# Two layers of graph attention on one core: moving a strip's side work of TensorE by one or two steps

## The chip, the cores and the metric

The kernel runs on one core of a Trainium2 chip. The metric is the device time of one execution in microseconds (us). Before the change it is 4260.31 us, the median of 3 runs (4258.36 to 4260.47).

## What is computed

The input `x` is 8 batches of 2048 nodes with 256 features, in float32, and `adj` is a 2048 x 2048 adjacency. Each layer adds its result to the normalized and rectified input's residual path.

```python
# layer 0
h = relu(layernorm(x))
q, k, v = h @ Wq.T + bq, h @ Wk.T + bk, h @ Wv.T + bv     # 4 heads of 64
scores = clip(q k^T / 8, -10, 10); masked entries are -10
attn = softmax(scores) within each of 8 chunks of 256 keys # per chunk
ctx = sum over the chunks of attn @ v
out = layernorm(ctx @ Wo.T + bo + h) * gamma + beta
x = x + out
# layer 1
h = relu(layernorm(x)); q = h @ W
attn = softmax(mask(leaky_relu(e_src[i] + e_dst[j])))      # over all 2048 nodes
x = x + elu(attn @ q)
```

The change touches only layer 0. What matters of it is that each of the 8 chunks of a row has a softmax of its own, so that each chunk's weighted sum must be divided by its own denominator before it is added to the others.

## The kernel before

Layer 0 (`layer0_block`) works batch by batch. A batch has 4 strips of 512 query rows (`NS`), and a strip has 32 steps (`STEPS`): one for each of 8 chunks of keys and 4 heads, in the order that `chunk_and_head` gives. At the start of a strip, steps 0 and 1 are heads 0 and 1, and head 2 is first met in step 4. Batch 0 is written out, batches 1 to 6 are a hardware loop, and batch 7 is written out.

In a step, TensorE makes the scores (`scores`, L674 and L675: four matmuls of 512 columns) into one of three PSUM slots. ScalarE takes the exponential in place (L829). VectorE clips it against the mask into one of four `probs` buffers (L968), which frees the slot. TensorE multiplies with the values (`values`, L687: 32 small matmuls) into one of two `outs` buffers. VectorE inverts the denominators (L974) and scales the sums into one of four `parts` buffers (L989), or directly into `ctx_sum` for chunk 0. GpSimd adds the part to `ctx_sum` (L514).

The order of the work on each engine is written out by hand. TensorE issues the scores of two steps and then, after the odd one, the values of the two steps that lie three and two behind. The values of a step wait until the sums of the step two before have been scaled. VectorE in step i first inverts and scales step i - 3 (`BACK`), then clips step i, and then does its side work of that step.

The three slots are used in one rotation (`count_uses`), by the scores and by all side work of TensorE, in the order in which TensorE issues it. Whoever wants a slot waits until the use three places before has been released by VectorE.

The side work of TensorE in a strip, each with one use of a slot:

- `turn` at step 3 and `project` at step 5 finish the strip before (transpose of `ctx_sum`, output projection).
- `transposes` (L596): a pair of tiles of the next batch's normalized input is transposed, and VectorE's `relu_t` (L893) brings it to `h_t`. `T_AT` gives the steps of the strip before's tiles in strips 1, 2 and 3, and `T_LAST_AT` those of the last strip's tiles, in strip 3. The last batch has none.
- `queries` (L624): the queries of the next strip for a pair of heads, in strips 0, 1 and 2, at the steps of `Q_AT`. ScalarE converts half of the result (L798), and VectorE the rest (L923), both standing in their engine's order right in that step. Then SyncE copies the two heads' halves to the other partitions with two DMAs (L397, `copy_queries`). The next strip's step 0 waits for the copies of heads 0 and 1, and its step 4 for those of heads 2 and 3.

GpSimd also makes the residual of each transposed pair (`residual`, L480 and L482), two steps ahead of `T_AT` by its own count.

The strips' side work that other engines have in the same steps stays at fixed steps: VectorE has statistics at 18 and 19, and normalizes tiles at 22 to 25 (strips 1 to 3), and in strip 0 at 18 to 21 and at 28 to 31.

Layer 1 (`layer1_block`) follows after layer 0 and holds none of the changed code.

Of the kernel before, what the change touches and what calls it, by code (L numbers as in the profile page):

```python
# [41 lines left out]
STEPS = NC * H  # L42
# [39 lines left out]
TURN_AT = 3  # L82
W_AT = 5
BACK = LAG + 1
T_AT = (26, 29)
T_LAST_AT = (10, 13)
Q_AT = (STEPS - 4, STEPS - 1)
GROUP = 2 * H
Q_AFTER_V = (3, 5)
W_MUL_AT = (8, 12)  # L90
# [23 lines left out]
def t_pairs(s):  # L114

    pairs = {}
    if s > 0:
        pairs.update({i: (s - 1, pair) for pair, i in enumerate(T_AT)})
    if s == NS - 1:
        pairs.update({i: (s, pair) for pair, i in enumerate(T_LAST_AT)})  # L120
    return pairs
# [7 lines left out]
def count_uses(last):  # L129
# [3 lines left out]
    def use(*name):  # L133
        place[name] = len(place)

    for s in range(NS):
        for i in range(STEPS):
# [5 lines left out]
            if i in t_pairs(s) and not last:  # L143
                use("t", *t_pairs(s)[i])
            if i in Q_AT and s < NS - 1:
                use("q", s + 1, Q_AT.index(i))
            if i in T1_AT and s == NS - 1 and last:
# [47 lines left out]
def layer0_block(nc, x, adj, wq_t, bq, wk_t, bk, wv_t, bv, wo_t, bo, gamma, beta, w, a, x1, mask_dram, s_dram, d_dram, both):  # L195
    with ExitStack() as ctx:
# [114 lines left out]
        def used(b, kind, *name):  # L311

            place = USES[kind][name]
            skipped = 2
            if kind == FIRST:
                skipped = sum(place >= USES[kind][(gone, 0)] for gone in ("turn", "project"))
            return b * BATCH_USES + PROLOGUE_USES - skipped + place

        def spot(kind, *name):

            return slots[used(0, kind, *name) % SLOTS]
# [9 lines left out]
        def acted(b, s, i):  # L331

            queries = sum(at < i for at in Q_AT) if s < NS - 1 else 0
            ahead_of_it = sum(at < i for at in P1_AT) if isinstance(b, int) and b == B - 1 and s == NS - 1 else 0
            return PROLOGUE_ACTS + b * BATCH_ACTS + s * STRIP_ACTS + i + queries + ahead_of_it + 1

        def acted_query(b, s, qu):

            return PROLOGUE_ACTS + b * BATCH_ACTS + s * STRIP_ACTS + Q_AT[qu] + qu + 2

# [13 lines left out]
        def tiles(s):  # L354

            return slice(s * IT, (s + 1) * IT)
# [88 lines left out]
        def _(pool):  # L445
# [24 lines left out]
            def inverse_std(n, strip):  # L470

                pool.wait_ge(moments_done, n)
                nc.gpsimd.tensor_tensor(rstd[:, strip], moments[:, strip, 1], eps_s[:, strip], ALU.add).then_inc(var_eps_done, 1)
                pool.wait_ge(var_eps_done, n)
                nc.gpsimd.tensor_tensor(rstd[:, strip], rstd[:, strip], neg_half[:, strip], ALU.pow).then_inc(rstd_done, 1)
# [41 lines left out]
            def batch(b, kind):  # L517
                first, last = kind == FIRST, kind == LAST
                for s in range(NS):
                    has_before = s > 0 or not first  # L520
                    before = (b, s - 1) if s > 0 else (b - 1, NS - 1)
                    for i in range(STEPS):
# [20 lines left out]
                        if s > 0 and not last:  # L543
                            if i == 17:
                                inverse_std(b * NS + s + 2, tiles(s - 1))
                            if i + BACK - 1 in T_AT:
                                pair = T_AT.index(i + BACK - 1)
                                pool.wait_ge(slot_filled, used(b, kind, "t", s - 1, pair) + 1)
# [20 lines left out]
        def _(pe):  # L569
# [50 lines left out]
            def queries(strip, qu, use, slot):  # L620

                fill(use)
                for c in range(KC):
                    last = nc.tensor.matmul(slot[:, 0, :], wq_s[:, c, qu * P:(qu + 1) * P],  # L624
                                            h_t[:, c, strip * STRIP:(strip + 1) * STRIP],
                                            start=(c == 0), stop=(c == KC - 1))
                last.then_inc(slot_filled, 1)
# [34 lines left out]
            def batch(b, kind):  # L662
# [30 lines left out]
                for s in range(NS):  # L693
                    has_before = s > 0 or not first
                    for i in range(STEPS):
# [11 lines left out]
                        if i in t_pairs(s) and not last:  # L707
# [4 lines left out]
                                       used(b, kind, "t", strip, pair), spot(kind, "t", strip, pair))  # L712
                        if i in Q_AT and s < NS - 1:
                            qu = Q_AT.index(i)
                            queries(s + 1, qu, used(b, kind, "q", s + 1, qu), spot(kind, "q", s + 1, qu))
# [1118 lines left out]
```

## Time and profile before

| | |
|---|---|
| time, median of 3 runs | 4260.31 us |
| the profiled execution's own time | 4262.97 us |
| its span, from the first to the last instruction | 4261.2 us |
| TensorE busy with matmuls | 91% |
| VectorE busy | 86% |
| ScalarE busy | 62% |
| GpSimd busy | 59% |
| mean granted TensorE clock | 0.987 |

The shares are averages over both layers. The last scores of layer 0 start at 2756.6 us of the span. The timeline of one engine shows when each instruction started and how long it took; a wait is printed in brackets behind the instruction that it held up, with the instruction that ended it.

### The profile page before, as it was taken

How to read it: one execution, taken by the hardware profiler on the slowest of the kernel's cores; microseconds unless marked ns; L12 is line 12 of the kernel's file. 1: busy time of each engine (PE TensorE's matmuls, PEld its weight loads, DVE VectorE, ACT ScalarE, POOL GpSimd, SP SyncE). 2: the span in 40 equal slices, each digit the busy share in tenths (PEclk: the TensorE clock that was granted, in tenths of full speed). 3: DMA queues.
4: the chain of work that ended last, by engine and by line, in shares of the span. 5: the costliest groups of instructions: out<-in, count | busy, mean ns of one | idle time of the engine just before them, and what ended most of it. 6: DMA issues, size and time to landing. Idle time of an engine off the chain costs nothing. (4 is left out here: it accounts for less than half of the span.)

```text
span 4261.2 us, 167542 instructions
## 1 busy us (share of the span) xinstructions
PE 3896.9 (91%) x72712; PEld 3242.9 (76%) x72712; DVE 3667.4 (86%) x6086; ACT 2656.7 (62%) x2960; POOL 2514.0 (59%) x1881
## 2 busy tenths in 40 slices
PE   6999999999999999999999999968889888888977
PEld 4877877777777777777787787757778787777877
DVE  5888888788788788788788888789999999999998
ACT  5665555555555555555565555457777777777776
POOL 4453554355345345354354353377988889888887
PEclk9999999999999999999999999989999999999999
DMA  6010010110101011010011010121221212122121
GB/s 129 29 30 23 27 32 22 37 32 22 34 26 32 27 32 32 28 27 27 22 37 32 22 30 22 34 66 26 87 70 43 85 35 82 55 61 75 40 67 38
DMA packets 170001, 178.75 MB, mean 42 GB/s; under 512 B 7184, under 2 KB 157072, under 8 KB 169104
## 3 DMA queue, kind: packets, MB, share of 16 engines
q1 hardware_dynamic: 166144, 156.08, 13.0%
q0 software_dynamic: 3088, 11.54, 1.3%
q8 instruction: 590, 9.67, 1.0%
q14 instruction: 179, 1.47, 0.1%
HBM read 107.02 MB, written 34.62 MB: 33 GB/s over the span
## 5 line engine op out<-in xcount | busy, mean ns | idle before, releaser
L829 ACT ACTIVATE slot<-slot,shift 128x1024 f32<-128x1024 f32 x1024 | 1077.2, 1085 | 931.4 <-PE slot L675 930.2
L514 POOL TENSOR_TENSOR ctx_sum<-ctx_sum,parts 128x256 f32<-128x256 f32 x896 | 651.0, 735 | 1325.5 <-DVE parts L989 1325.1
L968 DVE SCALAR_TENSOR_TENSOR probs<-slot,bound 128x1024 f32<-128x1024 f32 x1024 | 1242.7, 1217 | 94.2 <-ACT slot L829 88.3
L687 PEld LDWEIGHTS outs<-v_s,probs 128*64 128x64 f32 x32768 | 1007.5, 137 | 243.5 <-issue 166.6
L687 PE MATMUL outs<-v_s,probs 128*64 128x66 f32 x32768 | 1090.9, 223 | 42.7 <-DVE parts L989 31.0
L1597 ACT ACTIVATE t_ps<-s_all,d_rel 128x1024 f32<-128x1024 f32 x832 | 921.1, 1117 | 292.3 <-DVE p_dve L1710 277.4
L1710 DVE SCALAR_TENSOR_TENSOR p_dve<-t_ps,b_small,mask 128x1024 f32<-128x1024 f32 x832 | 1046.0, 1275 | 61.6 <-ACT t_ps L1597 60.6
L674 PE MATMUL slot<-q_hl,k_hl 128*128 128x512 f32 x2048 | 882.7, 431 | 28.5 <-DVE probs L968 21.0
L1439 POOL TENSOR_SCALAR p_pool<-r_all,b_big,b_small 128x1024 f32<-128x1024 f32 x192 | 746.5, 3888 | 141.7 <-ACT r_all L1589 141.6
L675 PE MATMUL slot<-q_hl,k_hl 128*128 128x512 f32 x2048 | 805.0, 393 | 0.0
L1500 PE MATMUL sums<-h_q_s,p_dve 128*64 128x66 f32 x13312 | 459.3, 226 | 113.9 <-DVE p_dve L1710 55.2
L1500 PEld LDWEIGHTS sums<-h_q_s,p_dve 128*64 128x64 f32 x13312 | 423.3, 140 | 156.1 <-DVE p_dve L1710 77.1
L674 PEld LDWEIGHTS slot<-q_hl,k_hl 128*128 128x128 f32 x2048 | 384.0, 188 | 149.8 <-DVE probs L968 39.8
L989 DVE TENSOR_TENSOR parts<-outs,inv 128x256 f32<-128x256 f32 x896 | 380.3, 424 | 120.5 <-POOL ctx_sum L514 34.8
L675 PEld LDWEIGHTS slot<-q_hl,k_hl 128*128 128x128 f32 x2048 | 385.4, 188 | 76.7 <-issue 11.5
L1442 POOL TENSOR_TENSOR p_pool<-p_pool,mask 128x1024 f32<-128x1024 f32 x192 | 411.1, 2141 | 16.0
L1500 PE MATMUL sums<-x_q_s,p_dve 128*64 128x66 f32 x6656 | 234.7, 229 | 73.5 <-DVE p_dve L1710 35.5
L789 ACT ACTIVATE bound<-mask,low 128x1024 f32<-128x1024 uint8 x256 | 293.9, 1148 | 0.8
L1500 PEld LDWEIGHTS sums<-x_q_s,p_dve 128*64 128x64 f32 x6656 | 218.1, 143 | 94.3 <-issue 40.7
L1500 PE MATMUL sums<-near,p_dve 128*64 128x66 f32 x6656 | 232.8, 228 | 53.1 <-DVE tail L1716 28.1
L1500 PEld LDWEIGHTS sums<-near,p_dve 128*64 128x64 f32 x6656 | 215.6, 142 | 71.0 <-DVE tail L1716 30.2
L798 ACT ACTIVATE q_hl<-slot,bq_s 64x512 fp32r<-64x512 f32 x128 | 87.4, 683 | 167.1 <-PE slot L624 166.3
(149 smaller groups left out, 4002.2 us busy)
## 6 DMA issues: line engine op xcount, KB each, us to landing
q_hl<-q_hl SPq DMA_DIRECT2D x128, 256.0 KB, 3.6
s_all<-s_turned SPq DMA_DIRECT2D x64, 512.0 KB, 5.6
x_q_s<-in_x SPq DMA_DIRECT2D x32, 512.0 KB, 4.7
x<-y SPq DMA_DIRECT2D x32, 512.0 KB, 3.1
t_o_s<-x SPq DMA_DIRECT2D x16, 1024.0 KB, 5.6
out<-t_o_s SPq DMA_DIRECT2D x16, 1024.0 KB, 8.5
x_q_s<-x SPq DMA_DIRECT2D x28, 512.0 KB, 7.1
probs<-in_adj POOLq DMA_DIRECT2D x12, 512.0 KB, 6.1
```

The source lines that it names most:

```text
L514: nc.gpsimd.tensor_tensor(ctx_sum[:, :, h, :], ctx_sum[:, :, h, :], parts[:, adds_before(i) % PARTS, :, :], ALU.add).then_inc(ctx_added, 1)
L674: nc.tensor.matmul(slot[:, r, :], kt, q_hl[:, h, 0, :], start=True, stop=False)
L675: end = nc.tensor.matmul(slot[:, r, :], kt, q_hl[:, h, 1, :], start=False, stop=True)
L687: end = nc.tensor.matmul(outs[i % OUTS][rows_of, q, 0:V_COLS], probs[:, i % PROBS, r, q * P + g * D:q * P + (g + 1) * D], v_s[:, c * JC + ...
L829: nc.scalar.activation(slot[:, :, :], slot[:, :, :], ACT.Exp, bias=shift[:, 0:1], scale=SCALE).then_inc(act_done, 1)
L968: nc.vector.scalar_tensor_tensor(probs[:, i % PROBS, :, :], spot(kind, "step", s, i)[:, :, :], P_LOW, bound[:, c % 2, :, :], ALU.max, ALU. ...
L989: nc.vector.tensor_tensor(parts[:, part % PARTS, :, :], outs[i % OUTS][:, :, 0:D], inv[:, i % 2, :].unsqueeze(2).to_broadcast([P, IT, D]), ...
L1439: nc.gpsimd.tensor_scalar(pp[:, n % PRING, :], r_all[:, m % HALVES, :], b_big[:, b % 2, j, h:h + 1], b_small[:, b % 2, j, h:h + 1], ALU.mu ...
L1442: nc.gpsimd.tensor_tensor(pp[:, n % PRING, :], pp[:, n % PRING, :], mask16[:, k, first:first + HALF], ALU.mult).then_inc(pp_made, 1)
L1500: last = nc.tensor.matmul(acc, left[:, t * P + g * D:t * P + (g + 1) * D], q_h, start=(j == 0 and t in (0, MAIN)), stop=(j == NT - 1), ski ...
L1597: nc.scalar.activation(t_ps[:, n % TRING, :], s_all[:, m % HALVES, :], ACT.Exp, bias=d_rel[:, b % 2, j, h:h + 1], scale=0.8).then_inc(t_ma ...
L1710: nc.vector.scalar_tensor_tensor(p[:, n % RING, :], t_ps[:, n % TRING, :], b_small[:, b % 2, j, h:h + 1], mask8[:, j, first:first + HALF], ...
```

## The change

Three tuples of step numbers change. All code that reads them follows: the order on TensorE, VectorE, ScalarE and GpSimd, the rotation of the slots and the semaphore counts.

```diff
@@ -82,9 +82,9 @@
 TURN_AT = 3
 W_AT = 5
 BACK = LAG + 1
-T_AT = (26, 29)
-T_LAST_AT = (10, 13)
-Q_AT = (STEPS - 4, STEPS - 1)
+T_AT = (25, 27)
+T_LAST_AT = (11, 13)
+Q_AT = (STEPS - 3, STEPS - 1)
 GROUP = 2 * H
 Q_AFTER_V = (3, 5)
 W_MUL_AT = (8, 12)
```

With it the two transposes of a strip move from steps 26 and 29 to 25 and 27, the first of strip 3's other pair from 10 to 11, and the first query projection from 28 to 29. The second projection stays at step 31. All of these are now odd steps, in which TensorE issues its side work after the values of a pair. VectorE's `relu_t` and both engines' conversions of the queries move with them, as do GpSimd's residuals (from steps 24 and 27 to 23 and 25).

## Rows read from the trace of the kernel before

**Rows 1.** The page: busy time (part 1), and a costly group (part 5: busy, idle, releaser).

```profile
PE 3896.9 (91%) x72712; PEld 3242.9 (76%) x72712; DVE 3667.4 (86%) x6086; ACT 2656.7 (62%) x2960; POOL 2514.0 (59%) x1881
...
L514 POOL TENSOR_TENSOR ctx_sum<-ctx_sum,parts 128x256 f32<-128x256 f32 x896 | 651.0, 735 | 1325.5 <-DVE parts L989 1325.1
```

**Rows 2.** Timeline of TensorE, end of a strip 2: start us, us, instruction, [idle before].

```profile
1305.36 0.50 PE L674 MATMUL slot<-q_hl,k_hl 128*128 128x512 f32 x1 [0.37 <-DVE probs L968]
...
1306.49 2.09 PE L687 MATMUL outs<-v_s,probs 128*64 128x66 f32 x64
...
1309.54 1.88 PE L624 MATMUL slot<-t_o_s,wide_s 128*128 128x512 f32 x4
...
1316.33 0.50 PE L674 MATMUL slot<-q_hl,k_hl 128*128 128x512 f32 x1 [0.45 <-DVE probs L968]
...
1319.47 1.98 PE L624 MATMUL slot<-t_o_s,wide_s 128*128 128x512 f32 x4
1320.89 0.80 PE L674 MATMUL slot<-q_hl,k_hl 128*128 128x512 f32 x1
...
1323.22 1.16 PE L687 MATMUL outs<-v_s,probs 128*64 128x66 f32 x32
1325.23 1.15 PE L687 MATMUL outs<-v_s,probs 128*64 128x66 f32 x32 [0.85 <-DVE parts L989]
1326.32 0.50 PE L674 MATMUL slot<-q_hl,k_hl 128*128 128x512 f32 x1
```

**Rows 3.** Timelines of VectorE and ScalarE in the same stretch.

```profile
1322.91 1.51 DVE L923 SCALAR_TENSOR_TENSOR q_hl<-slot,bq_s,q_hl 64x512 fp32r<-64x512 f32 x2 [2.39 <-ACT q_hl L798]
1324.45 0.18 DVE L974 RECIPROCAL inv<-outs 128x4 f32<-128x4 f32 x1
1324.76 0.42 DVE L989 TENSOR_TENSOR parts<-outs,inv 128x256 f32<-128x256 f32 x1
...
1321.49 1.38 ACT L798 ACTIVATE q_hl<-slot,bq_s 64x512 fp32r<-64x512 f32 x2 [2.84 <-PE slot L624]
```

**Rows 4.** SyncE's copies L397, strip 2's first pair; last row: a strip 1's second.

```profile
L397 SPq DMA_DIRECT2D q_hl<-q_hl x2: 490/536/582, 1314.4 to 1315.0; - x2
...
DMA to landing us min/median/max: 3.1/3.4/3.7
...
DMA to landing us min/median/max: 3.1/4.1/5.0
```

**Rows 5.** Timeline of TensorE, a strip of the last batch.

```profile
2573.57 0.50 PE L674 MATMUL slot<-q_hl,k_hl 128*128 128x512 f32 x1
...
2574.60 1.88 PE L624 MATMUL slot<-t_o_s,wide_s 128*128 128x512 f32 x4
...
2579.35 0.50 PE L674 MATMUL slot<-q_hl,k_hl 128*128 128x512 f32 x1
...
2581.39 2.09 PE L687 MATMUL outs<-v_s,probs 128*64 128x66 f32 x64
2583.41 1.98 PE L624 MATMUL slot<-t_o_s,wide_s 128*128 128x512 f32 x4
```

**Rows 6.** Timeline of TensorE, steps 10 to 13 of a strip 3.

```profile
1347.45 0.50 PE L674 MATMUL slot<-q_hl,k_hl 128*128 128x512 f32 x1
...
1356.47 0.66 PE L596 MATMUL slot<-ident,ahead 128*128 128x128 f32 x4
...
1358.93 1.27 PE L687 MATMUL outs<-v_s,probs 128*64 128x66 f32 x36
```

**Rows 7.** Timeline of TensorE, steps 28 to 31 of a strip 0.

```profile
1155.00 0.50 PE L674 MATMUL slot<-q_hl,k_hl 128*128 128x512 f32 x1
...
1165.26 1.98 PE L624 MATMUL slot<-t_o_s,wide_s 128*128 128x512 f32 x4
```

**Rows 8.** Timeline of TensorE, both projections of the first batch's strip 0.

```profile
149.74 1.88 PE L624 MATMUL slot<-t_o_s,wide_s 128*128 128x512 f32 x4
158.55 1.98 PE L624 MATMUL slot<-t_o_s,wide_s 128*128 128x512 f32 x4
```

## The prediction

> **What bounds the kernel now.** I read the page first, then the order of each engine's work at the end of a strip, then the queue of SyncE. Part 1 shows TensorE as the fullest engine and VectorE behind it [rows 1]. The change moves only work of the first layer, so I read stretches of that layer in time order, and took each step's length as the distance between starts.
>
> TensorE issues two steps' scores and then the values of a pair. Where nothing intervenes the two scores take 2.04 us (2579.35 to 2581.39) and the pair's values 2.02 us (2581.39 to 2583.41) [rows 5]. That is 2.03 us per step, with no idle time: TensorE sets the pace. At a strip's end it does not. Call a step's number its place in the strip (0 to 31), S a step's scores, V(a,b) the values of steps a and b, T a transpose pair, Q a query projection. Now the order is S26 T S27 V(24,25) S28 Q0 S29 V(26,27) T S30 S31 V(28,29) Q1 S0' S1' V(30) V(31). In a strip with T and Q TensorE waits three times: 0.37 us at S27, 0.45 at S31, each for a clip that frees one of three slots, and 0.85 at V(31), for the scaled part of step 29 [rows 2]. The last is a chain through three engines: Q1 starts at 1319.47, ScalarE converts from 1321.49 to 1322.87, VectorE from 1322.91 to 1324.42 (having idled 2.39 us for it), then inverts and scales until 1325.18, and V(31) starts at 1325.23 [rows 2, 3]. So a projection standing right behind a pair's values costs 5.76 us from its start to the second next V, where unhindered work would need 1.42 + 2.33 + 1.01 = 4.76 (the starts 1319.47, 1320.89 and 1323.22, and half a pair's values). Today only Q1 is such; Q0, between S28 and S29, is waited for by nobody on TensorE: VectorE's turn after it is in time for V(28,29).
>
> **The change, part by part.** It moves instructions and adds none. The new order is S24 S25 V(22,23) T S26 S27 V(24,25) T S28 S29 V(26,27) Q0 S30 S31 V(28) V(29) Q1 S0' S1' V(30) V(31).
>
> *Transposes at 25 and 27.* A T behind values: 1356.47 to 1358.93 is 2.46 us for T and both scores, 0.42 over the bare 2.04 [rows 6]. The T between scores costs more, and S behind it waits for the clip two steps back. Does the first move end that wait? No. S27 still uses step 25's slot (the ring has three, T takes one), and VectorE ends clip 25 no earlier: S27 stays at 1305.36 and V(24,25) at 1306.49 [rows 2]. The second T then takes 0.42 before V(26,27) instead of after. VectorE's two small additions there (a T's relu ahead of the inversion) are covered by TensorE's T and V, if barely: by my estimate clip 27 ends within 0.1 us of S29's turn. If that cover fails each such strip loses a T's 0.4 us at most, 21 x 0.4 = 8 us.
>
> *Query 0 at 29.* From V(24,25) at 1306.49: 2.02 to T, 2.46 to V(26,27) at 1310.97, 2.02 to Q0 at 1312.99. Q0 is now of Q1's kind. ScalarE converts it behind the exponentials 28 and 29; VectorE blocks on it in step 29 with the inversion and scaling of step 27, the clip of 30 and all later ones behind it in its queue; V(29) needs that scaling. So V(29) starts at Q0 + 5.76 = 1318.75 instead of 1.01 behind V(28): a new wait of about 1.0 us. Q1 follows 1.09 later (as 1325.23 to 1326.32 [rows 2]), at 1319.84. Before it was at 1319.47. **A strip with T and Q loses 0.37 us**, though its waits at S31 and the dearer place of T are gone. Q1 stays at 31 and its own chain is as before, so V(31) moves by the same 0.37.
>
> How many: T and Q together stand in strips 1 and 2 of the first seven batches, 14 x 0.37 = 5.2 us.
>
> *Strips with queries only.* From S28 the new way is 2.04 + 2.02 + 5.76 + 1.09 = 10.91 us to Q1. Before, strip 0 took 1165.26 - 1155.00 = 10.26 [rows 7] and a strip of the last batch 2583.41 - 2573.57 = 9.84 [rows 5]. Strip 0 of batches 1 to 6 loses 0.65 each, 3.9 us in all. The three strips of the last batch lose 1.07 each; strip 0 of the first batch too, as its two projections stand 8.81 apart (149.74, 158.55 [rows 8]), like the last batch's (2583.41 less 2574.60): 4 x 1.07 = 4.3 us.
>
> *Strip 3.* At 25 and 27 its two T need the same sum of time, the wait at S27 stays, nothing else is late: 0. The T at 10 goes to 11: now S10 to the T at 13 takes 1356.47 - 1347.45 = 9.02 us [rows 6]. New: 2.04 + 2.02 + 2.46 + 2.02 = 8.54, and about 0.07 for clip 11 that S13 then just meets: a gain of 0.41, seven times, -2.9 us.
>
> *The copies.* Each query's halves are copied by two DMAs of SyncE's queue, and S0' waits for Q0's, S4' for Q1's. Nothing else is queued with them. The first is issued as VectorE ends, the second about 0.54 later (an issue takes 490 to 582 ns), and the later of the two lands 3.7 us after its issue [rows 4]. So Q0's are there at Q0 + 2.02 + 1.42 + 1.51 + 0.03 + 0.54 + 3.7 = Q0 + 9.2. Today that is 2.3 us before S0' asks (1309.54 + 9.1 against 1320.89). In the new order S0' is ready at Q0 + 6.85 + 1.42 = Q0 + 8.27, so it waits about 1 us. But V(31) comes at Q0 + 12.61 by VectorE's chain, and from S0' at 9.27 TensorE reaches it at 12.4: the wait is hidden, with 0.2 us to spare. The spare is small: a copy that lands late is paid. One copy landed 5.0 us after its issue [rows 4], 1.1 beyond the spare. I take this for one strip in twenty, 24 x 1.1 / 20 = 1.3 us, with 0 and 24 x 1.1 = 26 as bounds; 0 is the nearer, since the strip walked here has the 3.7.
>
> Under the Trainium skill, DMA: Bandwidth & Descriptors, in Anatomy of one DMA, a transfer costs about 2.0 us fixed plus its bytes at 436 GB/s, 2.6 us for these 256 KB. By it S0' would find the copies at Q0 + 8.1 and not wait at all. The trace has 3.1 to 3.7 us and decides. The same page's advice to issue early and wait late speaks against this change: Q0's copies leave 3.5 us later for the same reader.
>
> *GpSimd.* Its residual work moves to steps 23 and 25. It idles 1325 us for scaled parts over the first layer [rows 1] and four parts are buffered, so nothing: 0, and if two residuals in four steps did block a scaling, some tenths in 21 strips, at most the 0.2 spare on either side of V(29)'s wait, 4 us.
>
> **Sum:** 5.2 + 3.9 + 4.3 - 2.9 + 1.3 = 11.8 us. On the profiled execution (span 4261.2, its own time 4262.97) that gives 4274.8; it lies 2.7 above the median of the runs, 4260.31, from which I take **4272 us**.
>
> **Rivals.**
> (a) *The wait for the scaling doesn't appear* (ScalarE or VectorE reach Q0 in time, or V(29) has other cover). Then Q0 to Q1 is 1.42 + 2.33 + 2.02 = 5.77 instead of 6.85: strips with T and Q gain 0.71 each, strip 0 gains 0.43, the four others nothing; -9.9 - 2.6 - 2.9 = -15 us, 4245. For it: three waits and two dear places of T are what the reordering removes, 0.82 us a strip. Against: Q1 pays exactly this wait in each place where it stands so. It decides once the wait is under 0.6 us instead of 1.08 (6.85 less 5.77): 24 times the difference is the whole sum.
> (b) *The copy shows.* S0' waits beyond the spare in most of the 24 strips, by 0.5 to 1.0 us: 12 to 24 us more, 4284 to 4296. For it: a spare of 0.2 and one copy at 5.0. Against: the strip walked here, and a copy can be late by 0.2 for nothing.
> (c) *The parts nearly cancel*: the new wait is half as long, because S30 and S31 start early and something behind VectorE catches up. 0.3 to 0.5 less in 24 strips, 4260 to 4265. Against it: the chain from Q0 to the scaling has no slack at any of its steps.
> (d) *The order isn't felt*, because VectorE paces the strip's end: its busy share there would be full; it idles over 2 us for Q1. Little.
>
> **Chances.** Forecast (4267 to 4277): 0.68. (b) 0.12, (c) 0.11, (a) and (d) 0.09. A change below 0.2%, 8.5 us, can't be told from none. The forecast lies 3 us above that bound and its lower edge inside it, so: slower 0.76, within 0.16, faster 0.08. For eight in ten: 4260 to 4285; it leaves out (a) and the worse half of (b).
>
> **What would show it.** Right: the waits at S31 gone, that at S27 left; a new wait of about 1.0 us before V(29), put down to the scaled part, in 24 strips; TensorE's wait for VectorE's parts up by some 20 us in the list of waits; S0' waiting about 1 us, for the q copy; Q1 later by 0.37, 0.65 and 1.07 us from the same anchor in the three kinds; the T at 13 of strip 3 earlier by 0.4; the second layer as long as before. Wrong: V(29) right behind V(28), or V(31) released by its scores instead of by the part, or a strip's length down.

## The result and the profile after

The changed kernel takes 4274.61 us, the median of 7 runs (4270.86 to 4281.79), against 4260.31 us before (7 runs, 4253.09 to 4264.56). The ratio of the runs is 1.0036, with a 95% interval of 1.0025 to 1.0048: slower by 0.36%, 14 us. The forecast was 4272 us.

The engines' busy times differ by 0.2% at most from [rows 1] (TensorE 3903.8 us against 3896.9), so the time is in the waits. The two profiled executions have spans of 4261.2 and 4271.5 us, 10.3 apart. They are cut in three below: until the first `turn` of TensorE (step 3 of the first batch's strip 1), until its last (behind layer 0's last step), and the rest. Columns: the stretch and its length; the busy time of TensorE's matmuls, its weight loads, VectorE, ScalarE and GpSimd, each with its number of instructions; the granted clock of TensorE, the busy share of the DMA engines and GB/s. Before:

```profile
0.00:169.46 169.46, 133.40 (x1633) 102.60 (x1633) 109.38 (x211) 97.02 (x103) 66.60 (x97) 0.98 0.41 88
169.46:2763.28 2593.82, 2518.91 (x37613) 2005.04 (x37609) 2148.84 (x4169) 1466.72 (x1482) 1196.81 (x1315) 1.00 0.10 29
2763.28:4261.20 1497.92, 1244.56 (x33471) 1135.29 (x33471) 1409.18 (x1707) 1093.01 (x1375) 1250.56 (x469) 0.97 0.21 59
```

After:

```profile
0.00:165.45 165.45, 132.66 (x1633) 101.34 (x1633) 109.22 (x211) 96.94 (x103) 66.70 (x97) 0.98 0.41 90
165.45:2775.36 2609.91, 2523.82 (x37612) 2003.90 (x37609) 2149.49 (x4169) 1464.44 (x1482) 1198.04 (x1315) 1.00 0.10 29
2775.36:4271.50 1496.14, 1247.31 (x33471) 1139.71 (x33471) 1406.89 (x1707) 1093.33 (x1375) 1252.39 (x469) 0.96 0.20 59
```

The middle, in which all but the first of the moved pieces stand, is 16.1 us longer (2609.91 against 2593.82), at the same granted clock (1.00). Layer 1 is 1.8 us shorter and holds no changed code. The start is 4.0 us shorter, by two parts. The first `L624` of all, which is ahead of any changed code, starts at 77.31 us instead of 82.97, 5.7 us earlier. From there to the first `turn`, where the first batch's strip 0 has its moved projection, it takes 1.65 us more (88.14 against 86.49). One strip shows the mechanism, the end of a strip 2 in TensorE's timeline, which answers to [rows 2]:

```profile
1306.54 0.50 PE L674 MATMUL slot<-q_hl,k_hl 128*128 128x512 f32 x1 [0.42 <-DVE probs L968]
...
1307.66 2.09 PE L687 MATMUL outs<-v_s,probs 128*64 128x66 f32 x64
1309.68 0.66 PE L596 MATMUL slot<-ident,h_q_s 128*128 128x128 f32 x4
...
1312.13 2.09 PE L687 MATMUL outs<-v_s,probs 128*64 128x66 f32 x64
1314.15 1.98 PE L624 MATMUL slot<-t_o_s,wide_s 128*128 128x512 f32 x4
1315.57 0.79 PE L674 MATMUL slot<-q_hl,k_hl 128*128 128x512 f32 x1
...
1317.91 1.15 PE L687 MATMUL outs<-v_s,probs 128*64 128x66 f32 x32
1319.92 1.16 PE L687 MATMUL outs<-v_s,probs 128*64 128x66 f32 x32 [0.85 <-DVE parts L989]
1321.01 1.98 PE L624 MATMUL slot<-t_o_s,wide_s 128*128 128x512 f32 x4
1324.76 0.49 PE L674 MATMUL slot<-q_hl,k_hl 128*128 128x512 f32 x1 [1.77 <-DMA q_hl<-q_hl]
```

V(24,25) is the line at 1307.66, Q0 at 1314.15, V(29) at 1319.92 with its new wait, Q1 at 1321.01, and S0' at 1324.76 behind a wait for the copies. V(29) starts 2.01 us behind V(28), where half a pair's values takes 1.01: its start is 1.0 us late, of which 0.85 is printed, since a wait is counted from the end that the profile models for the matmul before. V(29) waits so in all 24 strips. The wait of 0.45 us at S31 is gone, that at S27 is there still. VectorE in the same place, which shows who holds V(29) up:

```profile
1317.59 1.51 DVE L923 SCALAR_TENSOR_TENSOR q_hl<-slot,bq_s,q_hl 64x512 fp32r<-64x512 f32 x2 [2.18 <-ACT q_hl L798]
1319.13 0.18 DVE L974 RECIPROCAL inv<-outs 128x4 f32<-128x4 f32 x1
1319.44 0.42 DVE L989 TENSOR_TENSOR parts<-outs,inv 128x256 f32<-128x256 f32 x1
```

It idles 2.18 us for ScalarE's half of the conversion, converts, and only then scales step 27's sums, until 1319.86; V(29) starts 0.06 later.

Two other places, the last batch's strip and strip 0, from S28 to Q1:

```profile
2582.42 0.50 PE L674 MATMUL slot<-q_hl,k_hl 128*128 128x512 f32 x1
...
2586.49 1.98 PE L624 MATMUL slot<-t_o_s,wide_s 128*128 128x512 f32 x4
...
2592.26 1.15 PE L687 MATMUL outs<-v_s,probs 128*64 128x66 f32 x32 [0.85 <-DVE parts L989]
2593.34 1.12 PE L624 MATMUL slot<-t_o_s,wide_s 128*128 128x512 f32 x2
```

```profile
1155.20 0.50 PE L674 MATMUL slot<-q_hl,k_hl 128*128 128x512 f32 x1
...
1165.03 1.15 PE L687 MATMUL outs<-v_s,probs 128*64 128x66 f32 x32 [0.84 <-DVE parts L989]
1166.12 1.12 PE L624 MATMUL slot<-t_o_s,wide_s 128*128 128x512 f32 x2
```

Both take 10.92 us, where before it was 9.84 [rows 5] and 10.26 [rows 7].

The copies, in the strip shown first and in a strip 1 (SyncE's line L397: durations in ns, starts; who waited; time from issue to landing):

```profile
L397 SPq DMA_DIRECT2D q_hl<-q_hl x2: 489/536/582, 1319.1 to 1319.7; - x2
...
  PE slot L674: 1.8, 1
...
DMA to landing us min/median/max: 3.1/4.0/5.0
```

```profile
L397 SPq DMA_DIRECT2D q_hl<-q_hl x2: 467/528/590, 1241.7 to 1242.2; - x2
...
  PE slot L674: 0.5, 1
...
DMA to landing us min/median/max: 3.1/3.4/3.7
```

In the first the later copy needed 5.0 us and TensorE waited 1.77; in the second 3.7, and it waited 0.48. What that costs stands below.

### The profile page after: what moved, and what is told of

The parts are those of the page before. It is cut to its first block and busy times, and to the rows that moved or that the text cites. A ratio compares the mean times of both kernels' runs of the same rounds, so it can differ in the third digit from the quotient of the medians.

```text
span 4271.5 us, 167578 instructions
## 1 busy us (share of the span) xinstructions
PE 3903.8 (91%) x72712; PEld 3244.9 (76%) x72712; DVE 3665.6 (86%) x6086; ACT 2654.7 (62%) x2960; POOL 2517.1 (59%) x1881
## 3 DMA queue, kind: packets, MB, share of 16 engines
q1 hardware_dynamic: 166144, 156.08, 12.7%
## 5 line engine op out<-in xcount | busy, mean ns | idle before, releaser
L687 PE MATMUL outs<-v_s,probs 128*64 128x66 f32 x32768 | 1093.6, 223 | 43.3 <-DVE parts L989 29.9
L674 PE MATMUL slot<-q_hl,k_hl 128*128 128x512 f32 x2048 | 871.4, 425 | 40.8 <-DMA q_hl<-q_hl 15.6
```

Of the source, the lines that this page charges most:

```text
L674: nc.tensor.matmul(slot[:, r, :], kt, q_hl[:, h, 0, :], start=True, stop=False)
L687: end = nc.tensor.matmul(outs[i % OUTS][rows_of, q, 0:V_COLS], probs[:, i % PROBS, r, q * P + g * D:q * P + (g + 1) * D], v_s[:, c * JC + ...
```

## The experiments

Each was run against the kernel before on the same chip. S, V, T and Q are as in the prediction.

**e1: the first projection back at step 28.**

```diff
-Q_AT = (STEPS - 3, STEPS - 1)
+Q_AT = (STEPS - 4, STEPS - 1)
```

> The changed kernel with its first projection back at step 28 (transposes at 25 and 27, and 11 and 13, stay). Theory (the loss is the first projection's conversion, which VectorE must finish before it scales the part that V(29) waits for): that wait of 0.85 us is gone in all 24 strips, V(24) to Q1 in a strip with transposes and queries is 2.02 + 2.46 + 1.70 + 2.02 + 2.04 + 2.02 = 12.26 us instead of 12.98 before, so 14 x 0.72 + 7 x 0.4 = 13 us under the kernel before: about 4247 us. Rival (the transposes behind values cost, through VectorE's relu ahead of an inversion): it stays at 4265 to 4275. Rival (only the copies cost): at 4260, no gain from the transposes.

Measured: 4248.95 us, ratio 0.9973 (0.9962 to 0.9984). The transposes alone make the kernel faster, by 11 us where 13 were expected. From one `turn` to the next, the fourteen strips with T and Q lie 0.65 to 0.86 us under those of the kernel before, the strips with queries only within 0.05. The rivals that laid the loss on the transposes or on the copies alone fall.

**e2: the first projection alone at step 29.**

```diff
-Q_AT = (STEPS - 4, STEPS - 1)
+Q_AT = (STEPS - 3, STEPS - 1)
```

(in the kernel before, `T_AT` and `T_LAST_AT` as they were)

> The kernel before with only the first projection moved to step 29 (transposes at 26 and 29, and 10 and 13, as before). Theory: the whole loss and none of the gain of strip 3's early transpose: 0.37, 0.66 and 1.07 us in 14, 6 and 4 strips, 13.5 us, and about 1 us for each late copy in a quarter of the strips, 5 us: about 4279 us. Rival (transposes are the cost): about 4260.

Measured: 4282.51 us, ratio 1.0048 (1.0031 to 1.0065). The projection's move carries the loss. That e2 is slower than the changed kernel is what it lacks of strip 3's gain (1.3 us over seven strips) and, in the profiled executions, more late copies: 8 of 24 first copies landed 4.5 us or more after their issue, 6 in the changed kernel. The two parts don't add up: e1's gain in strips with T and Q is not in the changed kernel. Those strips are 0.3 to 0.4 us longer than before both in e2 and in the changed kernel, where the copies are in time. Once V(29) waits for the part, the transposes' places in front of it no longer matter; only strip 3's stay a gain.

**e3: VectorE converts one place later.** Built on the changed kernel.

```diff
                             scale(s, i - BACK)
+                        if pending:
+                            queries(*pending)
+                            pending = None
                         if i < STEPS:
                             clip(s, i)
...
-                            queries(qu, acted_query(b, s, qu), spot(kind, "q", s + 1, qu))
+                            pending = (qu, acted_query(b, s, qu), spot(kind, "q", s + 1, qu))
```

> The changed kernel, but VectorE converts each projection one place later in its own order: behind the inversion and scaling of the next step instead of ahead of them. Theory: both waits for the scaled part (V(29) and V(31), about 1.0 us each) are gone, but S0' now waits for the copies of the first projection, which still land at Q0 + 9.2 while S0' is ready at Q0 + 7.2: a wait of 2.1 us for the DMA in every strip, and V(31) comes only 0.2 to 0.3 us earlier than in the changed kernel: 5 to 7 us under it, about 4268. Rival (the copies have room, VectorE's order is all): 24 x 2.0 = 48 us under it, about 4226.

Measured: 4269.12 us, ratio 1.0019 (1.0008 to 1.003), 5.5 us under the changed kernel. The timeline of TensorE, a strip 1:

```profile
1235.60 1.98 PE L624 MATMUL slot<-t_o_s,wide_s 128*128 128x512 f32 x4
...
1239.37 2.09 PE L687 MATMUL outs<-v_s,probs 128*64 128x66 f32 x64
1241.39 1.98 PE L624 MATMUL slot<-t_o_s,wide_s 128*128 128x512 f32 x4
1244.91 0.49 PE L674 MATMUL slot<-q_hl,k_hl 128*128 128x512 f32 x1 [1.54 <-DMA q_hl<-q_hl]
1246.94 2.09 PE L687 MATMUL outs<-v_s,probs 128*64 128x66 f32 x64
```

Both pairs of values now run through (x64, no wait), Q1 follows Q0 by 5.79 us instead of 6.85, and S0' starts at Q0 + 9.31, where the copies land. The wait that the list of waits lays on the copies grows from 15.6 us to 29.5. Of 2.0 us a strip that the two waits had taken, the copies take back all but 0.35. So in the changed kernel the copies stood right behind VectorE's chain, hidden by it: V(31) starts at Q0 + 12.33 here, where only the copies hold it up, and at Q0 + 12.61 there.

**e4: the same edit on e1.**

> e1 with VectorE's conversion behind the scaling of the next step, as in e3. The first projection stands at 28, so its copies leave 3 us earlier and nobody waits for them. Theory: V(31)'s wait of 0.85 us goes and nothing takes its place but about 0.1 us for a clip: 24 x 0.9 = 21 us under e1, about 4226 us. Rival (something else is due at the same time, as the exponential of the next strip's first step, which stands behind a bound on ScalarE): no better than e1.

Measured: 4251.88 us, ratio 0.9982 (0.9972 to 0.9991): a miss. The wait is gone and the time is not. TensorE in e1, from Q1 to the `turn` of the next strip:

```profile
1309.65 1.98 PE L624 MATMUL slot<-t_o_s,wide_s 128*128 128x512 f32 x4
...
1315.42 1.15 PE L687 MATMUL outs<-v_s,probs 128*64 128x66 f32 x32 [0.85 <-DVE parts L989]
...
1320.59 0.66 PE L635 MATMUL slot<-ident,ctx_sum 128*128 128x128 f32 x4
```

and in e4:

```profile
1306.79 0.50 PE L674 MATMUL slot<-q_hl,k_hl 128*128 128x512 f32 x1 [0.19 <-DVE q_hl L923]
...
1309.94 1.98 PE L624 MATMUL slot<-t_o_s,wide_s 128*128 128x512 f32 x4
...
1317.14 0.50 PE L674 MATMUL slot<-q_hl,k_hl 128*128 128x512 f32 x1 [0.24 <-DVE probs L968]
...
1320.63 0.55 PE L635 MATMUL slot<-ident,ctx_sum 128*128 128x128 f32 x3
```

From Q1 to `turn` it is 10.94 us in e1 and 10.69 in e4: of 0.85 us only 0.25 are left. S3' waits for clip 0' (1317.14). And S31 waits now for the first projection's slot (0.19), which VectorE frees later: from Q0 to Q1 it is 9.30 us against 8.81 (1300.64 and 1300.84 are the Q0 of the two), which takes back more than the 0.25. ScalarE in e4 shows why clip 0' is late:

```profile
1311.96 1.38 ACT L798 ACTIVATE q_hl<-slot,bq_s 64x512 fp32r<-64x512 f32 x2 [2.84 <-PE slot L624]
1313.37 1.15 ACT L789 ACTIVATE bound<-mask,low 128x1024 f32<-128x1024 uint8 x1
1314.54 2.09 ACT L829 ACTIVATE slot<-slot,shift 128x1024 f32<-128x1024 f32 x2
```

It idles 2.84 us for Q1, converts, makes the next strip's bound, and only then takes the exponential of S0'. The bound could fill the idle time. That is the rival of e4's expectation, and it led to the next three.

**e5: e1 with VectorE's second conversion later and ScalarE's bound earlier.** The first conversion stays where e1 has it. On ScalarE:

```diff
+                        if i == STEPS - 1 and s < NS - 1:
+                            make_bound(s + 1, 0, used(b, kind, "step", s, step_at(NC - 2, H - 1)))
                         if i in Q_AT and s < NS - 1:
                             qu = Q_AT.index(i)
                             queries(qu, used(b, kind, "q", s + 1, qu), spot(kind, "q", s + 1, qu))
...
-                    if s < NS - 1:
-                        make_bound(s + 1, 0, used(b, kind, "step", s, step_at(NC - 2, H - 1)))
```

> e1 with two edits: VectorE converts the second projection behind the scaling of the next step (the first as before), and ScalarE makes the next strip's first bound before it converts the second projection instead of after. Theory from the trace of e4: V(31)'s wait had only been one of two that end within 0.1 us; the other is ScalarE's bound (1.15 us) ahead of the exponential of S0', whose clips hold up S3' and V(1'). With both gone the next strip's turn comes 0.8 to 1.1 us earlier in 24 strips: 19 to 26 us under e1, 4223 to 4230 us. Rival (the bound is not it): like e1, 4249.

Measured: 4221.67 us, ratio 0.9909 (0.9893 to 0.9926). It beats both kernels, by 39 us and by 53, and lies 27 us under e1, where 19 to 26 were expected. TensorE:

```profile
1297.15 1.98 PE L624 MATMUL slot<-t_o_s,wide_s 128*128 128x512 f32 x4
...
1300.90 2.09 PE L687 MATMUL outs<-v_s,probs 128*64 128x66 f32 x64
...
1304.96 2.09 PE L687 MATMUL outs<-v_s,probs 128*64 128x66 f32 x64
1306.97 1.09 PE L635 MATMUL slot<-ident,ctx_sum 128*128 128x128 f32 x8
```

No wait stands between Q1 and `turn`, 9.82 us.

**e6: e1 with the bound alone earlier.**

> e1 with the second of those edits alone (bound before the conversion). Theory: V(31) still waits 0.85 us for the scaled part, so the same time as e1, within 2 us of 4249. Rival (ScalarE's bound alone was the limit): 15 us or more under e1.

Measured: 4248.79 us, ratio 0.9973 (0.9962 to 0.9983): the same as e1. The bound alone is not the limit, as long as V(31) waits for the part.

**e7: e1 with the second conversion alone later.**

> e1 with the first of those edits alone (second projection's conversion behind the scaling). Theory: V(31) doesn't wait, but clip 0' comes no earlier, so S3' and V(1') give it back; the 0.25 us a strip that e4 lost at S31 aren't lost: 4247 to 4250. Rival: e4's missing gain lay in the first projection's later conversion alone, then 15 us or more under e1.

Measured: 4239.17 us, ratio 0.995 (0.9933 to 0.9966). A miss: 4247 to 4250 was expected, the same as e1. Its strips with queries are mostly 0.2 to 0.3 us shorter than e1's (0.5 in the last batch), 6 us in all; 0.25 is what e4's own rows show behind Q1. The medians are 10 us apart; the other 4 us are in no strip's length that I compared. e7 differs from e4 only in the first projection's conversion, which stands early again, and is 12.7 us faster. So the rival of e7's expectation held in part: what e4 lacked lay in that conversion and in the bound. From e7 to e5 the strips lose mostly another 0.8 to 0.9 us each. By the medians the two edits give 10 us and nothing alone, and 27 together; by the strips' lengths 6, nothing and 25.

**e9: the first of Q0's copies in two halves.** Built on the changed kernel.

```diff
-                    sp.dma_start(q_hl[other, 2 * qu + r, :, :].bitcast(F32), q_hl[own, 2 * qu + r, :, :].bitcast(F32))\
-                        .then_inc(q_copied[qu], 16)
+                    for part in (slice(0, 1), slice(1, 2)) if qu == 0 and r == 0 else (slice(0, 2),):
+                        sp.dma_start(q_hl[other, 2 * qu + r, part, :].bitcast(F32), q_hl[own, 2 * qu + r, part, :].bitcast(F32))\
+                            .then_inc(q_copied[qu], 16)
```

> The changed kernel, but the first of the two copies of each first projection is issued as two DMAs of half the size, so that the last of now three is issued, and should land, about 0.5 us later. Theory (the copy's wait of 0.49 us at S0' is hidden behind VectorE's scaling with 0.1 us to spare): S0' waits about 1.0 us, V(31) no more, and each of 24 strips is 0.4 us longer: 10 us over the changed kernel, about 4284. Rival (S0' isn't on the path, the copy has room): no change, 4274.

Measured: 4278.88 us, ratio 1.0044 (1.003 to 1.0059), which the interval does not tell from the changed kernel's. It did not do what it was made for, a later landing, so it decides nothing between its theory and its rival. (An earlier form of it, e8, which issued the first copy twice, has no measured time.) Its lines from L398 on are those of the others plus one. SyncE's line in a strip 1:

```profile
L398 SPq DMA_DIRECT2D q_hl<-q_hl x3: 467/582/590, 1245.0 to 1246.1; - x3
...
  PE slot L675: 0.4, 1
...
DMA to landing us min/median/max: 2.2/2.4/2.9
```

The last was issued 1.1 us after the first and landed 2.9 to 3.0 us later, no later than before. TensorE in that strip:

```profile
1249.19 0.49 PE L675 MATMUL slot<-q_hl,k_hl 128*128 128x512 f32 x1 [0.37 <-DMA q_hl<-q_hl]
1252.60 1.15 PE L688 MATMUL outs<-v_s,probs 128*64 128x66 f32 x32 [0.24 <-DVE parts L990]
```

S0' waits 0.1 us less than in the changed kernel, V(31) that much more, and the strip is as long (77.47 us from one `turn` to the next against 77.45). That agrees with a hidden copy. What a later copy costs is seen where one happens to be late: in the strip 2 shown for the changed kernel S0' starts at Q0 + 10.61 instead of 9.32, 1.29 us later, and the strip is 0.97 us longer (78.41 from `turn` to `turn`, against 77.44 in a strip 2 whose copy is in time).

## Why the prediction was right

**The new wait.** Forecast: V(29) at Q0 + 5.76, Q1 at Q0 + 6.85. Measured: 1319.92 - 1314.15 = 5.77, and 6.86. From V(24) to Q1 it is 1321.01 - 1307.66 = 13.35 us, the figure of the forecast; before it was 12.98. From S28 to Q1 10.92 against a forecast of 10.91, in both other kinds of strip. e1 and e2 show the cause from both sides, and e3 shows that VectorE's order makes the wait.

**The transposes.** That they give nothing in a strip with a late Q0 was right. The wait at S27 stayed (0.42), as predicted, with clip 25 no earlier. In strip 3 the move from 10 to 11 gave less than the 0.41 us forecast:

```profile
1349.96 0.50 PE L674 MATMUL slot<-q_hl,k_hl 128*128 128x512 f32 x1
...
1354.02 0.66 PE L596 MATMUL slot<-ident,ahead 128*128 128x128 f32 x4
...
1356.64 2.09 PE L687 MATMUL outs<-v_s,probs 128*64 128x66 f32 x64
1358.66 0.55 PE L596 MATMUL slot<-ident,ahead 128*128 128x128 f32 x3
```

8.70 us against 9.02 before [rows 6]: 0.32. From T to the values there are 2.62 us, not the 2.46 of the sum: the second score meets clip 11, and that took 0.16 where I had put 0.07.

**The copies.** They were ready where forecast (S0' at Q0 + 9.32 in a strip with a landing of 3.7; forecast 9.2 to 9.3) and hidden. The spare is 0.3 us, not the 0.2 of the forecast: V(31) is at Q0 + 12.61 with VectorE's chain and at 12.33 in e3 without it, and a copy that is 1.29 us late costs 0.97. The forecast's own rows give the same, as 9.27 + 2.04 + 1.01 is 12.32 and not 12.4. The 0.1 that is printed before V(31) is again less than the shift of its start. The forecast's estimate of 2.6 us a copy, by the Trainium skill, DMA: Bandwidth & Descriptors, Anatomy of one DMA, uses a fit that the page gives for DMAs issued from GpSimd; these are issued from SyncE, and the traces have 3.1 and 3.7.

The number of late copies was mis-sized; this is the term that was off: one in twenty, 1.3 us in all. In the profiled execution 6 of 24 first copies landed so late that S0' waited 1.4 to 1.8 us. One was in the first batch's strip 0, the other five in strips 2, and these five strips are 0.7 to 1.0 us longer than the others of their kind, 4.2 us in all. In the kernel before it was 1 of 24, so one in twenty fits that kernel; it did not carry over to a projection one step later.

What goes with a late copy can be read from the traces. In four of the six strips 2 that lie in the hardware loop, a packet of the instruction queue (16 KB) began 2.6 to 3.1 us after the first of the two copies was issued, and these four are the late ones. In the fifth it began after 3.6 us and the copy took 3.8; in the sixth it came after the landing. In the other twelve strips there was none. The same holds for the nine kernels that issue two copies at a time, over all 576 pairs of copies in their traces: in 97 such a packet began 2.0 to 3.2 us after the first issue, and the later copy took 4.5 us or more in every one; in the other 479 it took at most 4.6. That it is the packet that delays the copy was not tried.

**The sum of the middle stretch**, from one `turn` to the next:

| | forecast | measured |
|---|---|---|
| 14 strips with T and Q, copies in time | 5.2 | 14 x 0.36 = 5.0 |
| 6 strips 0 | 3.9 | 4.2 |
| 3 strips of the last batch | 3.2 | 3.4 |
| late copies | 1.3 | 4.2 |
| strip 3 and what follows it, 7 times | -2.9 | -1.7 |
| last strip, a stop of TensorE with no change near it | - | 1.0 |
| sum | 10.7 | 16.1 |

The forecast's remaining 1.1 us is the first batch's strip 0, ahead of this stretch; it measured 1.65, with the sixth late copy in it. In the seven strips 3 one is longer by 0.3 instead of shorter by 0.35: a copy at the batch's end landed after 6.7 us. So the places with changed code cost 16.7 us in the profiled executions (16.1 and 1.65, less the stop of 1.0), against 11.8 forecast. The forecast was low by the late copies, 3.5 us, and by strip 3, 1.2 us. The medians are 14 us apart, which agrees with the forecast of 12 within the runs' spread; that they agree better than the terms do is in part luck.

**The list of waits** was expected to show some 20 us more for VectorE's parts. It shows 29.9 us against 31.0 before, no more. V(29) waits 0.85 in 24 strips, but V(31)'s 0.85 shrank to 0.2 or less, since S0' now waits for the copy in front of it (15.6 us in the list, and 5.2 more in the first and last batch that stand under "issue"). That S0' would wait about 1 us was right by its start: 9.32 against the 8.27 at which it is ready behind Q1, with 0.48 printed. The strip's length is set by VectorE's chain all the same. The step was right and the sign to look for was wrong: I had worked out that the copy's wait is hidden, and did not see that it takes the other wait's place in the list.

**The rivals.** (a) is excluded by the waits at V(29), (d) by e1, (c) by the strips' lengths, which differ from the forecast by less than 0.1 us where the copies are in time, but for one strip 0 with 0.15. (b) came in part: in 6 of 24 strips.

## What to carry to other kernels

A piece of work that must pass through three engines in a row, each with an order of its own, costs what the slowest path back to its first engine costs; count the distance from its issue to the next instruction that needs what the last engine does after it. Two such pieces in a strip are best placed so that other work, and not that path, lies behind them (e1), and the engine that waits should do first what others need from it (e5). Before taking a wait away, look for what is due within a microsecond of it: here one edit alone gave 10 us, another nothing, and both together 27.

## What the runs showed of the hardware

A copy between partitions of 256 KB in one DMA landed 3.1 us after its issue, and the next one, issued 0.5 us later, after 3.7, in most strips. Cut into three DMAs, with the last issued 1.1 us after the first, the same 512 KB landed no later (Q0 + 9.1 against Q0 + 9.2). Where a 16 KB packet of the instruction queue began 2.0 to 3.2 us after the first issue, the later copy took 4.5 us or more, in 97 of 97 cases over nine kernels; in the changed kernel 4.5 to 5.1 in most, and up to 6.7 at a batch's end. Four of its six late first copies stand at the same place of the program in different batches.
